# Raw rows of x gathered in the prologue for nine half units, their messages computed in the counting stage

## The reference

```python
hs, hd = h[src], h[dst]
e = jnp.concatenate([hs, hd], axis=1)
a1 = jnp.exp(jax.nn.relu(e @ W_att_1 + b_att_1))        # a2, a3 alike
att1 = jax.ops.segment_sum(a1, dst, num_segments=N)     # att2, att3 alike
avg_a = (a1 / att1[dst] + a2 / att2[dst] + a3 / att3[dst]) / 3.0
m = avg_a * relu(relu(relu(hs @ W_msg_1 + b_msg_1) @ W_msg_2 + b_msg_2) @ W_msg_3 + b_msg_3)
deg = segment_sum(ones, dst)
h_neigh = jax.ops.segment_sum(m, dst, num_segments=N) / jnp.maximum(deg, 1.0)
out = relu(concat([h, h_neigh]) @ W_c1 + b_c1) @ W_c2 + b_c2
x = _layernorm(x + out)
```

## Time and profile before

| | |
|---|---|
| median of three runs | 826.16 us |
| the profiled execution | 826.97 us |
| its span | 822.9 us |
| busy: PE, DVE, POOL, ACT | 656.1 us (80%), 577.4 (70%), 590.9 (72%), 381.7 (46%) |
| indirect DMAs of POOL (L1154) | 594, 566.4 us busy, 191.8 us of idle time before them |
| mean granted TensorE clock | 0.809 of full speed |

### The profile page before, as it was taken

The page is one execution under the profiler, slowest core; times in us unless marked ns, Lnnn a source line. Parts: engine busy times, 40 slices in busy tenths (PEclk is TensorE's granted clock), DMA queues, the critical chain, the costliest instruction groups (busy, mean ns, idle before and its releaser), DMA issues.

```text
span 822.9 us, 16893 instructions
## 1 busy us (share of the span) xinstructions
PE 656.1 (80%) x4917; PEld 512.9 (62%) x4917; DVE 577.4 (70%) x1934; ACT 381.7 (46%) x999; POOL 590.9 (72%) x638
## 2 busy tenths in 40 slices
PE   9945677777578778989898988888877978878885
PEld 5734455544345446778787877776666766667664
DVE  4882656585688877677776767775577868787766
ACT  5522555463444443677676767662123322333323
POOL 7437777777777777777777777777777777777770
PEclk9975555567565675799999999999699989998989
DMA  6533222225652233333333333334233443443421
GB/s 190 142 105 69 63 65 65 65 65 57 71 65 62 62 92 78 74 87 76 80 82 75 83 78 84 77 77 131 65 90 102 112 108 102 104 130 101 98 58 35
DMA packets 79474, 70.44 MB, mean 86 GB/s; under 512 B 34040, under 2 KB 65312, under 8 KB 79376
## 3 DMA queue, kind: packets, MB, share of 16 engines
q0 software_dynamic: 19008, 39.88, 22.2%
q1 hardware_dynamic: 60080, 29.28, 13.3%
q10 hardware_dynamic: 288, 0.13, 0.1%
HBM read 62.32 MB, written 6.90 MB: 84 GB/s over the span
## 4 chain that ended last, share of the span: by engine, by line
POOL 35%; DVE 21%; issue 19%; PE 17%; ACT 4%; DMA 2%; DVEq 2%; ACTq 0%; SPq 0%; POOLq 0%
POOL work L1154 34%; DVE fin L1561 4%; PE bank L1281 4%; DVE acc L1668 3%; ACT bank L1383 3%; DVE counts L1539 2%; DVE fin L1526 2%; DVE fin L927 2%; PE bank L836 2%; PE bank L565 2%; PE bank L544 2%; DMA work<-message_table,src_t 1%; PE bank L1285 1%; PE bank L1319 1%; DVE side L1592 1%
## 5 line engine op out<-in xcount | busy, mean ns | idle before, releaser
L1154 POOL DMA_INDIRECT work<-message_table,src_t x594 | 566.4, 953 | 191.8 <-issue 178.0
L1281 PE MATMUL bank<-work 128*128 128x144 f32 (+8 forms) x1188 | 248.7, 343 | 66.5 <-DVE acc L1668 66.4
L1281 PEld LDWEIGHTS bank<-work 128*128 128x128 f32 x1188 | 197.7, 234 | 100.4 <-issue 86.0
L1444 ACT COPY work<-bank 128x192 f32<-128x192 f32 (+7 forms) x126 | 37.4, 297 | 250.9 <-DVE work L1634 246.5
L1319 PE MATMUL bank<-work,fin 128*128 128x129 f32 (+1 forms) x882 | 117.3, 290 | 0.0
L1668 DVE TENSOR_TENSOR acc<-acc,bank 128x192 f32 (+8 forms) x297 | 88.7, 299 | 31.3 <-issue 7.5
L1319 PEld LDWEIGHTS bank<-work,fin 128*128 128x128 f32 (+1 forms) x882 | 108.2, 201 | 2.5 <-issue 0.6
L1383 ACT ACTIVATE bank<-hot_logit 128x384 f32<-128x384 f32 (+1 forms) x147 | 72.7, 494 | 70.9 <-DVE fin L1561 62.0
L1651 DVE TENSOR_TENSOR work<-bank,work 128x576 f32<-128x576 f32 (+7 forms) x126 | 86.2, 684 | 13.1
L1285 PE MATMUL bank<-work 128*4 128x48 f32 (+8 forms) x1188 | 95.0, 207 | 0.0
L1561 DVE SCALAR_TENSOR_TENSOR fin<-bank,counts 128x384 f32<-128x384 f32 (+1 forms) x147 | 81.4, 554 | 18.1 <-ACT bank L1383 17.4
(11 more groups left out here) (132 smaller groups left out, 688.9 us busy)
## 6 DMA issues: line engine op xcount, KB each, us to landing
work<-message_table,src_t POOLq DMA_INDIRECT x594
side<-near_nodes SPq DMA_DIRECT2D x102, 48.0 KB
side<-logit_parts SPq DMA_DIRECT2D x297, 0.8 KB
message_table<-work SPq DMA_DIRECT2D x12, 262.0 KB, 3.4
work<-message_table SPq DMA_DIRECT2D x48, 65.5 KB
work<-in_x_t SPq DMA_DIRECT2D x12, 256.0 KB, 3.3
fin<-in_x SPq DMA_DIRECT2D x11, 256.0 KB, 2.9
logits_or_x<-in_x_t SPq DMA_DIRECT2D x11, 256.0 KB
```

What stands on the lines that cost most here:

```text
L1154: pool.indirect_dma_start(out=rows_of(n)[:, t, :], out_offset=None, in_=table[:, :], in_offset=bass.IndirectOffsetOnAxis(ap=src_t[:, h, g: ...
L1281: pe.matmul(sums[:, at:at + HEADS * w], rows_here[:, t, 0:P], wt_of(i)[:, t, :], start=h == 0, stop=h == TILES - 1)
```

## The change

Nine of the long units, 4, 6, 8, ... 20, are "early" (`early_units`). The second half of each (two groups, four tiles) is no longer gathered from the message table in the edge pass. Instead:

- In the prologue POOL gathers raw rows of x for these 36 tiles, into three staging areas in turn, and SP stores each set of four tiles to a new DRAM tensor `early_table` between the table's own stores. Their part of `src_t` is loaded first, by a DMA of its own.
- In the counting stage, over two steps for each early half, SP loads a set back, PE turns it (four transposes), ACT copies it out, PE and ACT run layers 1 and 2, PE layer 3, DVE adds the bias into the half's place in `gath`, and ACT applies the ReLU. The source logits are accumulated by PE onto the target part in `edge_q`.
- Bank 3, one of the two that `edge_q` took in turn, is given to this work. In the long units `edge_q` uses bank 1 alone, so it waits for `weights` of the unit before, and it stands behind `count_edges` in its step now.
- What POOL cleared in the prologue is partly moved to ACT: 1,000 words a chunk instead of 766, eight pieces after the last chunk, and the five pieces of `counts` at the start of the edge pass.

```diff
+EARLY = 9
+EARLY_FROM, EARLY_EVERY = 4, 2
...
+        early_h, early_x, EARLY_BANK = staged[2], staged[1], 3
...
+        ACT_WORDS, POOL_FIRST, POOL_LAST = 1000, 2000, 3200
...
+                STORE_AT = {0: [0], 2: [1], 3: [2], 5: [3], 6: [4], 8: [5], 10: [6], n_chunks - 1: [7, 8]}
+                def store_early(k):
+                    sp.wait_ge(s_staged[k % THREE], 16 * CHUNK * (k // THREE + 1))
+                    sp.dma_start(early_table[k * P:(k + 1) * P, :], staged[k % THREE]).then_inc(s_kept[k % THREE], 16)
...
-                pool.memset(acc_flat[:, 0:by_pool], 0.0).then_inc(s_zero, 1)
...
+                pool.memset(acc_flat[:, 0:POOL_FIRST], 0.0).then_inc(s_zero, 1)
+                pool.wait_ge(s_early_src, 16)
+                for k, groups in enumerate(early_groups):
+                    if k >= THREE:
+                        pool.wait_ge(s_kept[k % THREE], 16 * (k // THREE))
+                    for j, g in enumerate(groups):
+                        for h in range(TILES):
+                            at = (j * TILES + h) * P
+                            pool.indirect_dma_start(
+                                out=staged[k % THREE][:, at:at + P], out_offset=None, in_=x[:, :],
+                                in_offset=bass.IndirectOffsetOnAxis(ap=src_t[:, h, g:g + 1], axis=0),
+                            ).then_inc(s_staged[k % THREE], 16)
+                pool.memset(acc_flat[:, POOL_FIRST:act_from], 0.0).then_inc(s_zero, 1)
...
+            def q_bank(i):
+                return Q_BANKS[0] if i < n_long else Q_BANKS[i % TWO]
...
                         for j, g in enumerate(u):
+                            if j >= pair and early(n) is not None:
+                                continue
...
+                    def load_early(k):
+                        if k == 0:
+                            for j in range(THREE):
+                                sp.wait_ge(s_kept[j], 16 * len(range(j, EARLY, THREE)))
+                        else:
+                            sp.wait_ge(s_e3, k)
+                        sp.dma_start(early_h, early_table[k * P:(k + 1) * P, :]).then_inc(s_ein, 16)
...
                         one_hot_ready(pe, i)
-                        if i >= TWO:
-                            pe.wait_ge(s_wt, i - TWO + 1)
+                        if q_user(i) >= 0:
+                            pe.wait_ge(s_wt, q_user(i) + 1)
+                        elif first and q_bank(i) == EARLY_BANK:
+                            pe.wait_ge(s_erow, EARLY)
+                        k = early(i)
+                        if k is not None:
+                            pe.wait_ge(s_ecopy, k + 1)
                         for t in range(n_tiles(i)):
+                            mine = k is not None and t >= CHUNK
...
+                            if mine:
+                                last = pe.matmul(from_q(i)[:, t, 0:HEADS],
+                                                 early_x[:, (t - CHUNK) * P:(t - CHUNK + 1) * P], w_logit[:, 0:HEADS],
+                                                 start=False, stop=True)
...
+                    def turn_early(k):
+                        pe.wait_ge(s_ein, 16 * (k + 1))
+                        if k >= 1:
+                            pe.wait_ge(s_erow, k)
+                        for t in range(CHUNK):
+                            last = pe.transpose(bank[EARLY_BANK][:, t * P:(t + 1) * P], early_h[:, t * P:(t + 1) * P],
+                                                ident[:, :])
+                        last.then_inc(s_eturn, 1)
+                    def first_early(k):
+                        pe.wait_ge(s_ecopy, k + 1)
+                        pe.matmul(bank[EARLY_BANK][:, 0:COLS], w1, early_x, start=True, stop=True).then_inc(s_e1, 1)
+                    def second_early(k):
+                        pe.wait_ge(s_eh1, k + 1)
+                        pe.matmul(bank[EARLY_BANK][:, 0:COLS], w2, early_h, start=True, stop=True).then_inc(s_e2, 1)
+                    def third_early(k):
+                        pe.wait_ge(s_eh2, k + 1)
+                        for t in range(CHUNK):
+                            last = pe.matmul(bank[EARLY_BANK][:, t * P:(t + 1) * P], early_h[:, t * P:(t + 1) * P],
+                                             w3[:, :], start=True, stop=True)
+                        last.then_inc(s_e3, 1)
...
                         if i < n_units:
                             add_edges(i)
-                        if i + 2 < n_units:
+                        if i + 2 < n_units and not (first and i < COUNT_STEPS):
                             edge_q(i + 2)
+                        if k is not None and i % EARLY_EVERY == 0 and k >= 1:
+                            third_early(k - 1)
+                        if k is not None and i % EARLY_EVERY == 1 and k < EARLY:
+                            first_early(k)
                         if first and i < COUNT_STEPS:
                             count_edges(i)
+                        if k is not None and i % EARLY_EVERY == 0 and k < EARLY:
+                            turn_early(k)
+                        if k is not None and i % EARLY_EVERY == 1 and k < EARLY:
+                            second_early(k)
+                        if i + 2 < n_units and first and i < COUNT_STEPS:
+                            edge_q(i + 2)
...
+                    def copy_early(k):
+                        act.wait_ge(s_eturn, k + 1)
+                        if k >= 1:
+                            act.wait_ge(s_q, early_units[k - 1] + 1)
+                        act.copy(early_x, bank[EARLY_BANK][:, 0:COLS]).then_inc(s_ecopy, 1)
+                    def hidden_early(k, layer):
+                        ready, bias, made = ((s_e1, b1, s_eh1), (s_e2, b2, s_eh2))[layer]
+                        act.wait_ge(ready, k + 1)
+                        act.activation(early_h, bank[EARLY_BANK][:, 0:COLS], ACT.Relu, bias=bias).then_inc(made, 1)
+                    def relu_early(k):
+                        act.wait_ge(s_erow, k + 1)
+                        act.activation(early_rows(k), early_rows(k), ACT.Relu).then_inc(s_emsg, 1)
...
+                    def rows_early(k):
+                        dve.wait_ge(s_e3, k + 1)
...
+                        dve.tensor_tensor(early_rows(k), bank[EARLY_BANK][:, 0:COLS].rearrange("p (t f) -> p t f", f=P),
+                                          b3_all[:, :].unsqueeze(1).to_broadcast([P, CHUNK, P]),
+                                          ALU.add).then_inc(s_erow, 1)
```

142 lines of the change are left out of this document (104 added, 38 removed).

## The result

The changed kernel takes 830.25 us (median of 20 runs, 823.6 to 834.8); the kernel before took 824.92 us beside it (20 runs, 823.2 to 827.2). The ratio is 1.0052, 95% interval 1.0031 to 1.0073: 5.3 us slower. The forecast was 803 us, faster with a chance of 0.8.

What follows compares the result with a forecast made beforehand. The prediction took POOL's unbroken gather train as the floor, with consumers close behind and in places the bound. 826.97 + 1 (start) - 5 (counting) - 4 (hot) - 15 (tail) = 804, as median 803 us; range 782 to 830.

Steps and rivals of the forecast that it cites:

- POOL's train, 45.3 us: Edge pass: 36 gathers at 1.258 us each leave POOL's unbroken train, the most the change can give.
- The start, +1: Prologue and start of the edge pass: 1 us longer in all, range 0 to +4, +30 if gathers took 1.83 us.
- The counting stage, -5: Units 3 to 22: 195 us against 199.8, so 5 us gained.
- 19 x 10.1 + 3 = 195: Counting stage: 19 steps of 10.1 us, plus 3 us (0 to 14) for reloads that meet the logit stores.
- the forecast's own formula: Counting step: 9.2 us at full clock, 13 at half, weighted 0.67 and 0.33 for clock 0.83, giving 10.2 us.
- rival B: Counting stage: PE keeps the half clock, steps take 13 us, total 854 us; chance 0.18, wholly or in part.
- The tail, -15: Units after the hot stage: 15 of DVE's 20.0 us of waits for rows go, bounds 8 and 20.
- POOL arrives with a lead: Tail: POOL comes some 35 us ahead, gives back 20 us and doesn't become the bound again.
- waits on PE's sums (L1409) of 20 us or more in all: Sign expected on POOL if the forecast holds, where the kernel before has 2.4 us of waits.
- The hot stage, -4: Units 22 to 78: consumers' pace unchanged, 4 of the 4.6 us of waits for rows go.
- C: Rival, no change: the new order's loop takes what the slack gives, steps of 11.3 us, 827 us; chance 0.04.
- A: Rival, POOL stays the bound: full clock in counting, steps of 8.5 us or less, 782 us as median; chance 0.13.

Runs made afterwards that it cites:

- no_early_gath: Changed kernel with the prologue's 36 gathers replaced by plain copies of as many rows of x: 832.2 us, where the kernel before takes 825.0.
- skip_count_c: Kernel before with 36 gathers left out in units 4 to 20 and nothing in their place: 791.4 us beside 825.0.
- no_late: Kernel before without any gathers from unit 24 on: 803.8 us beside 825.0.
- before_again: Kernel before, unchanged, profiled on a slow chip: 999.2 us beside 999.4.
- ring6: Changed kernel with a ring of six places instead of eight, on a slow chip: 1032.1 us, where the kernel before takes 999.4.
- skip_late_b: Kernel before with 36 gathers left out, the last tile of each of units 24 to 59, on a slow chip: 948.4 us beside 996.8.

## Why the prediction was wrong

Its sum was +1 - 5 - 4 - 15. Measured: +1.9 + 5.5 - 4.7 - 3.7 (and +1.4 at the end).

1. **POOL's train, 45.3 us: right in size.** No gather became slower. Where it went was wrong, see 4.

2. **The start, +1: right.** The first table gather starts at 55.07 us (54.24 in before), and the weights of unit 3 come 1.9 us later, within the 0 to +4 of the forecast.

3. **The counting stage, -5: wrong.** The step that failed is "19 x 10.1 + 3 = 195". Sixteen of the nineteen steps took 10.2 us each, about as priced (steps 19 to 21 are among them, which have no early work any more and were priced with it). What was priced too low are three of them: steps 14, 16 and 18 took 40.7 us, and the forecast's three times 10.1 and its 3 us "for the reloads that meet the logit stores" are 33.3. Step 14 is such a reload, 6.0 us above the others; step 16 is a reload that SP issued late, 1.5 us above them. Step 18, 2.6 us above them, is DVE's, and was in the forecast at the price of any other step. `no_early_gath` repeats the three, with 39.5 us. The forecast's bound for the reload term, 14 us, was right; its value was not.
 The granted clock was wrong as well, 0.75 for 0.83. Put into the forecast's own formula it seems to explain everything: 1 / (0.5/9.2 + 0.5/13) is 10.77 us a step, 19 of them are 204.7, and 205.5 were measured. But that is a coincidence of means. The half level fell on the odd steps, which took 9.1 to 11.5 us and not 13, and the full one mostly on the even steps, of which six took 9.4 to 10.2 us and the three named 11.7 to 16.2, and not 9.2. The formula prices every step as the mean of an odd and an even one, and here each kind had a level of its own. One price inside it was too low too: at the full clock four groups of `add_edges` took 3.1 us (from 130.94 to 134.03), where halving the 5.0 us of the half clock gives 2.5. What a clock of 0.83 would have given, no run tells.
 In "TensorE: Matmul & The Clock Gate", Part 4, the Trainium skill says that transposes do not count as work for the clock gate as matmuls do. With the transposes in the stage the granted clock rose from 0.59 to 0.75, so rival B, half clock throughout, did not come; whether they kept it from rising further no run here tells. In steps 4, 6, 8 and 10 the clock was full at the transposes and half 1 to 3 us later (in step 6 it was 1.00 from 138.0 to 139.5 and 0.50 from 139.8 to 140.7, with the transposes at 138.0); that is a coincidence in time and shows no cause.

4. **The tail, -15: wrong, and this is the mechanism.** The step that failed is "POOL arrives with a lead: 45 us minus the 8 or so gained by then, and capped by the ring of eight short units", some 35 us. Measured: POOL began unit 78 at 561.9 us, 0.3 us earlier than in before. The ring of eight places was taken as a cap for the tail, where a place is one short unit. But the gathers were taken away in the counting stage, where a unit takes two places and the ring holds four units. There POOL was only 6.4 us short of it in before, a number that stood in the trace (sum of unit 20 at 285.5, gather of unit 24 at 291.9), and that the forecast didn't look up. What is taken from POOL beyond 6.4 us can't be carried past unit 24 unless the consumers get faster too. They got slower by 4 us, so that POOL begins unit 24 only 1.3 us earlier than before, and unit 28 no earlier at all. `skip_count_c` shows the rule without the added work: 33.5 us at the begin of unit 24, from a counting stage 27.6 us shorter and the 6 us of room.
 The sign that the forecast itself had named for this, "waits on PE's sums (L1409) of 20 us or more in all", came (49.6 us in the span), but it had been counted as the sign of a lead. A wait of the producer for a free place is the opposite: time that is lost for good. Its other sign did not come: the last gather was to start about 24 us earlier, and starts 1.3 us earlier.
 The two errors can be told apart by an estimate from these rows. With the forecast's 195 us in the counting stage and the ring as it is, unit 20 is summed 10.5 us earlier than in after, and everything behind it moves with it: 827.1 - 10.5, about 817 us. So the ring alone puts the forecast of 803 out of reach, and it is the counting stage's 10.5 us that leave the changed kernel without any gain.

5. **The hot stage, -4: right** (-4.7), and `no_late` gives the same 268.2 us.

6. **What isn't explained.** The profiled runs are level, and the medians 5.3 us apart. The runs of after spread over 11 us instead of 4. Their mean granted clocks lie between 0.844 and 0.861. The three runs with 0.858 or more took 823.7 to 825.8 us and the three with 0.844 took 830.0 to 832.0, but others (823.6 at 0.849, 831.7 at 0.857) don't fit. A stage whose pace hangs on which step meets which clock, or on when a reload lands, would spread like this, but that is argued, not shown. Open too are the 1.4 us that after takes longer from the weights of unit 125 to the span's end.

Of the rivals, C (no change, 827, chance 0.04) came nearest in time, with a step of 10.8 us on the average, and its reason was half of the truth: the new order and the early work took what the slack of the counting stage gave. The other half, the lead that was never there, was in none of them, so C's nearness is partly luck: its own step was 11.3 us, and steps of 10.8 lie in the forecast's band of 9.3 to 11, which it had paired with 788 to 818 us. A and B did not come. Faster had 0.80, and the range of 782 to 830 ended 0.25 us below the result.

## What to carry to other kernels

Before you relieve a producer, look up how far it was from being blocked by its ring at the last place where the relief ends: the sum of the holder against the producer's start on the same places. Beyond that distance a saving counts only as far as the consumers, in that very stage, get faster. And price added work step by step, not for a mean step: here two kinds of step met two clock levels, and three steps out of nineteen held most of the error, one of them by a reload that landed late.

## What the runs showed of the hardware

On the chips where the kernel before takes 985 to 1000 us, POOL's gathers are as long as elsewhere (950 ns in the mean, 953 in before on the first chip), and the prologue is the same to the microsecond (weights of unit 0 at 61.4, 61.8 in before). What differs begins with the first gathers. SP loads the logit parts of units by small DMAs (L1182), three of which, issued while POOL gathers, read so, first on the 825 us chip, then in `before_again`:

```profile
71.94 1.68 SPq L1182 DMA_DIRECT2D side<-logit_parts  x3
```

```profile
72.35 9.19 SPq L1182 DMA_DIRECT2D side<-logit_parts  x3
```

Three issues take 9.19 us instead of 1.68. Not all are slow: four later ones, from 96.61 us on, take 2.52 us. The near nodes that SP loads behind the slow ones come so late that DVE waits 23.9 us in one piece, and POOL waits in nearly every unit:

```profile
DVE side L1592 <- DMA side<-near_nodes: 23.9, 1, 23.9
```

```profile
POOL work L1154 <- remote: 170.7, 103, 5.0
```

("remote": the trace does not tell the update that ended the wait.) In the hot stage POOL begins a unit 4.9 to 5.0 us after PE's sum of the unit that held its place (units 50 to 70), and in `ring6`, with six places, 4.1 us after it. In after, on the first chip, it begins 0.3 us after the sum when it has waited for it. So POOL follows the freed place on these chips too, but late, and what passes in between no row shows. From unit 22 to 78 that kernel takes 357.9 us instead of 272.9. In `skip_late_b`, units with three gathers instead of four went at 4.7 us each (units 38 to 48), where `before_again` needs 6.1. So units go faster there with fewer gathers, though POOL's own 4 x 1.26 us don't fill the 6.1. A gather that costs the other engines time besides its own would explain this and what else was seen: 36 gathers are worth 43 to 48 us there at any place, and the changed kernel, which gathers in the prologue while SP stores the tables, loses 25.5 us before unit 3 (weights of unit 3 at 143.4 and 117.9 us) and nothing like it on the 825 us chip. It is argued and not shown that the gathers hold up SP or the others: `no_late` and `no_early_gath`, which would tell, ran on the 825 us chip only. Whether these are properties of the chips or of their state at the time is open too; one of them took 985.6 and, 37 minutes later, 984.8 us.
